# Two gathering layers turned from written-out instructions into hardware loops, with two steps in each PSUM bank

## The reference: what is computed

```python
xn = layernorm(x)
h = elu(gcn(xn, W1, b1)); h = elu(gcn(h, W2, b2))     # gcn: segment_sum((x @ W)[src] * norm, dst) + b
x = x + h + linear_attention(xn)                      # q, k = elu(.) + 1; context = k^T v; projection
x = x + moe(layernorm(x))                             # 8 experts of width 1024, the best 2 for each node
```

## Time and profile before

| | |
|---|---|
| time, median of 3 runs | 3330.49 us (3329.08 to 3338.45) |
| time of the profiled execution | 3338.05 us |
| its span in the profile | 3336.2 us |
| instructions | 45400 |
| TensorE busy | 2378.8 us, 71% |
| TensorE loading weights | 1766.3 us, 53% |
| VectorE busy | 1766.5 us, 53% |
| ScalarE busy | 619.5 us, 19% |
| GpSimd busy | 1965.2 us, 59% |
| DMA | 397.27 MB, mean 119 GB/s |

### The profile page before, as it was taken

One profiled execution on the slowest core, in us unless ns is written; L12 is line 12 of the kernel. 1 busy time (PEld: TensorE's weight loads), 2 busy tenths in 40 slices (PEclk: granted clock), 3 DMA queues, 4 the chain that ended last, 5 costly groups with the idle time before them and its releaser, 6 DMA issues. The chain is left out here.

```text
span 3336.2 us, 45400 instructions
## 1 busy us (share of the span) xinstructions
PE 2378.8 (71%) x10847; PEld 1766.3 (53%) x10847; DVE 1766.5 (53%) x4443; ACT 619.5 (19%) x1318; POOL 1965.2 (59%) x2107
## 2 busy tenths in 40 slices
PE   3367677767677767465666656666669399999998
PEld 2244444444444446243444434444448199999997
DVE  6144444444444456254445545555557766777765
ACT  2000000000000005010001101111116344444443
POOL 1666666666666653666666666666633045555554
PEclk9677877877888788676777777777789599999999
DMA  6333333333333322444444444444422465555551
GB/s 170 114 92 92 90 90 92 92 90 91 88 91 90 89 71 90 116 142 143 141 137 148 145 142 138 146 147 146 145 74 67 146 202 147 146 148 149 148 148 21
DMA packets 177904, 397.27 MB, mean 119 GB/s; under 512 B 42393, under 2 KB 96570, under 8 KB 169514
## 3 DMA queue, kind: packets, MB, share of 16 engines
q0 software_dynamic: 96800, 233.29, 26.9%
q1 hardware_dynamic: 50926, 103.38, 8.6%
q10 hardware_dynamic: 30012, 58.67, 5.1%
HBM read 322.87 MB, written 75.01 MB: 119 GB/s over the span
## 5 line engine op out<-in xcount | busy, mean ns | idle before, releaser
L644 POOL DMA_INDIRECT rows<-rows_layer,srcs x1564 | 1538.4, 984 | 767.6 <-issue 384.3
L705 PE MATMUL l_bank<-rows,sel 128*128 x3332 | 1190.7, 489 | 636.6 <-issue 228.4
L695 DVE TENSOR_TENSOR acc<-acc,l_bank 128x256 f32 x1666 | 699.1, 420 | 1237.2 <-remote 515.9
L705 PEld LDWEIGHTS l_bank<-rows,sel 128*128 128x128 f32 x3332 | 705.3, 236 | 997.2 <-issue 468.8
L1637 PE MATMUL ps_y<-whl,hhi 128*128 128x512 f32 x896 | 320.8, 398 | 0.0
L1593 POOL DMA_INDIRECT out<-ys,g_sum x112 | 182.2, 1627 | 198.1 <-DVE ys L1549 172.9
L673 DVE TENSOR_TENSOR sel<-iota_n,dloc 128x512 f32<-128x512 f32 x418 | 286.7, 686 | 20.1 <-issue 20.1
L1508 ACT ACTIVATE hr<-ffn_bank,vec 128x256 f32<-128x256 f32 x448 | 212.7, 475 | 375.9 <-PE ffn_bank L1449 335.4
L1447 PE MATMUL ffn_bank<-xh,whl 128*128 128x256 f32 x896 | 252.2, 281 | 2.4 <-DVE xl L1523 2.4
L1448 PE MATMUL ffn_bank<-xl,whl 128*128 128x256 f32 x896 | 252.2, 281 | 0.0
L1449 PE MATMUL ffn_bank<-xh,whl 128*128 128x256 f32 x896 | 252.0, 281 | 0.0
(11 more groups left out here) (273 smaller groups left out, 2240.8 us busy)
## 6 DMA issues: line engine op xcount, KB each, us to landing
whl<-w_hi SPq DMA_DIRECT2D x32, 1024.0 KB
whl<-w_lo SPq DMA_DIRECT2D x32, 1024.0 KB
rows<-rows_layer,srcs POOLq DMA_INDIRECT x1564
w_qkv<-wide ACTq DMA_DIRECT2D x49, 335.0 KB
w_hi<-whi ACTq DMA_DIRECT2D x49, 335.0 KB
w_lo<-wlo ACTq DMA_DIRECT2D x49, 335.0 KB
rows_layer<-acc SPq DMA_DIRECT2D x25, 256.0 KB, 2.1
rows_x<-acc SPq DMA_DIRECT2D x7, 910.0 KB
```

The lines of the kernel that those rows point to most:

```text
L644: pool.indirect_dma_start(rows[:, (n + 1) % ROWS, :], None, table[layer], bass.IndirectOffsetOnAxis(ap=srcs[:, n:n + 1], axis=0)).then_inc ...
L695: v.tensor_tensor(to, to, step_bank(s), ALU.add).wait_op(sem(f"summed{layer}"), s + 1, "sem-ge").then_inc(sem(f"added{layer}"), 1)
L705: t.matmul(step_bank(s), sel[:, s % SELS, :], rows_flat[:, bass.ds(slot * D, D)], start=True, stop=True).wait_op(sem(f"here{layer}"), t.to ...
```

## The change

The streams of TensorE, VectorE and SyncE for both layers, and ScalarE's work beside them, become hardware loops. The first turn, the 49th and the last 49 steps stay written out, with turns 2 to 48 in a loop of 16 steps each; SyncE loops over turns of 32 tiles; ScalarE loops over node tiles. Step numbers and the addresses that follow from them are computed in registers. GpSimd's 782 gathers for each layer stay written out.

Two steps share a PSUM bank: its halves hold the results of steps 2m and 2m + 1, so four banks hold eight results. TensorE waits for VectorE only ahead of an even step, until both results of the bank have been added. VectorE's add of an even step waits for both results, and that of an odd step only for the add before. The ring of 0/1 matrices grows from 12 to 16, made 10 steps ahead instead of 6, with three groups of four ahead of the first step.

```diff
--- before.py
+++ after.py
@@ -31,10 +31,12 @@
 PAIRS = -(-NT // 2)
 assert BLOCKS >= 2 * PAIRS + 2
 SG = -(-STEPS // P)
-ROWS, SELS, FOUR = 32, 12, 4
+ROWS, SELS, FOUR = 32, 16, 4
 LOADED = 4
 TURN = 16
 BEHIND, FREED_AT = 16, 8
+FULL_TURNS = (ET - ROWS + BEHIND) // ROWS
+assert ROWS % FREED_AT == 0 and BEHIND % FREED_AT == 0
 assert ROWS > BEHIND and ROWS & (ROWS - 1) == 0 and PAD_DST + NT < 1 << 16 and BLOCKS * D < 1 << 16 and ET < 1 << 16
 HEADS, HD = 8, 32
 NX, HID = 8, 1024
@@ -62,9 +64,11 @@
 WEIGHTS_AT = 9
 LN_EPS = 1e-5
 DEN_MIN = 1e-6
-AHEAD = 6
 PSB = 4
-assert AHEAD >= PSB + 2 and SELS == 3 * FOUR and STEPS <= SG * P - FOUR
+SUMS = 2 * PSB
+AHEAD = SUMS + 2
+assert AHEAD % FOUR == 2 and SELS >= AHEAD + FOUR + 2 and SELS == TURN and TURN % SUMS == 0
+assert STEPS + AHEAD + FOUR <= SG * P
 
 
 def gps_layer(nc, x, src, dst, wqkv, wproj, bproj, gw1, gb1, gw2, gb2, wr, br, wide, vectors, out):
@@ -645,89 +649,126 @@
                                         bass.IndirectOffsetOnAxis(ap=srcs[:, n:n + 1], axis=0)
                                         ).then_inc(sem(f"slot_{n % ROWS}"), 16)
 
-        def steps_until_free(n):
+        def steps_until_free(n, count):
 
             _, regs = nc.values_load_multi_w_load_instructions(
-                words[2:3, n + 1:min(n + FREED_AT, ET - ROWS) + 1, 0], engines=(SP_ENGINE,), min_val=1, max_val=STEPS,
+                words[2:3, bass.ds(n + 1, count), 0], engines=(SP_ENGINE,), min_val=1, max_val=STEPS,
                 skip_runtime_bounds_check_because="the first step of the next tile of edges")
             return list(regs)
 
         def tiles_here(sp, layer):
 
-            until = []
-            for n in range(ET):
-                sp.wait_ge(sem(f"slot_{n % ROWS}"), (n // ROWS + 1 + layer * -(-(ET - n % ROWS) // ROWS)) * 16)
-                sp.sem_inc(sem(f"here{layer}"), 1)
-                m = n - BEHIND
-                if 0 <= m < ET - ROWS:
-                    if m % FREED_AT == 0:
-                        until = steps_until_free(m)
-                    sp.wait_ge(sem(f"summed{layer}"), until[m % FREED_AT])
-                    sp.sem_inc(sem(f"freed{layer}"), 1)
+            def landed(j):
+                return layer * -(-(ET - j) // ROWS)
+
+            def turn(first, many, arrived):
+                until = []
+                for j in range(many):
+                    sp.wait_ge(sem(f"slot_{j}"), arrived(j))
+                    sp.sem_inc(sem(f"here{layer}"), 1)
+                    if isinstance(first, int):
+                        m = first + j - BEHIND
+                        freed, left = 0 <= m < ET - ROWS, ET - ROWS - m
+                    else:
+                        m, freed, left = first + (j - BEHIND), True, FREED_AT
+                    if freed:
+                        if j % FREED_AT == 0:
+                            until = steps_until_free(m, min(FREED_AT, left))
+                        sp.wait_ge(sem(f"summed{layer}"), until[j % FREED_AT])
+                        sp.sem_inc(sem(f"freed{layer}"), 1)
+
+            turn(0, ROWS, lambda j: (1 + landed(j)) * 16)
+            with sp.Fori(1, FULL_TURNS) as k:
+                values = {b: sp.snap(k * 16 + (1 + b) * 16) for b in sorted({landed(j) for j in range(ROWS)})}
+                turn(k * ROWS, ROWS, lambda j: values[landed(j)])
+            for k in range(FULL_TURNS, -(-ET // ROWS)):
+                turn(k * ROWS, min(ROWS, ET - k * ROWS), lambda j: (k + 1 + landed(j)) * 16)
 
         def step_bank(s):
-            return step_ps[s % PSB][:, 0:D]
-
-        def four_selects(v, layer, s):
-
-            v.tensor_tensor(sel[:, s % SELS:s % SELS + FOUR, :], iota_n[:, None, :].to_broadcast([P, FOUR, P]),
-                            dloc[:, s:s + FOUR, None].to_broadcast([P, FOUR, P]), ALU.is_equal
+            return step_ps[s // 2 % PSB][:, s % 2 * D:(s % 2 + 1) * D]
+
+        def four_selects(v, layer, first, k):
+
+            v.tensor_tensor(sel[:, k % SELS:k % SELS + FOUR, :], iota_n[:, None, :].to_broadcast([P, FOUR, P]),
+                            dloc[:, bass.ds(first + k, FOUR), None].to_broadcast([P, FOUR, P]), ALU.is_equal
                             ).then_inc(sem(f"selected{layer}"), 1)
 
-        def blocks_of(s):
+        def blocks_of(first, count):
 
             _, regs = nc.values_load_multi_w_load_instructions(
-                words[1:2, s:min(s + LOADED, STEPS), 0], engines=(DVE_ENGINE,), min_val=0, max_val=(BLOCKS - 1) * D,
+                words[1:2, bass.ds(first, count), 0], engines=(DVE_ENGINE,), min_val=0, max_val=(BLOCKS - 1) * D,
                 skip_runtime_bounds_check_because="a step's tile is one of the step's number or less, by less than the blocks")
             return list(regs)
 
-        def tiles_of(s):
+        def tiles_of(first, count):
 
             _, regs = nc.values_load_multi_w_load_instructions(
-                words[0:1, s:min(s + LOADED, STEPS), 0], engines=(PE_ENGINE,), min_val=1, max_val=ET,
+                words[0:1, bass.ds(first, count), 0], engines=(PE_ENGINE,), min_val=1, max_val=ET,
                 skip_runtime_bounds_check_because="a count of tiles, 1 to ET")
             return list(regs)
 
-        def step_add(v, layer, s, block):
-            if s > 0:
-                v.wait_ge(sem(f"added{layer}"), s)
+        def number(eng, n):
+            return n if isinstance(n, int) else eng.to_reg(eng.snap(n))
+
+        def step_add(v, layer, first, k, block, whole):
             to = acc[:, bass.ds(block, D)]
-            v.tensor_tensor(to, to, step_bank(s), ALU.add).wait_op(sem(f"summed{layer}"), s + 1, "sem-ge"
-                                                                   ).then_inc(sem(f"added{layer}"), 1)
-
-        def step_sum(t, layer, s, here):
+            if k % 2 == 0:
+                until = number(v, first + (k + 2 if whole else k + 1))
+                ins = v.tensor_tensor(to, to, step_bank(k), ALU.add).wait_op(sem(f"summed{layer}"), until, "sem-ge")
+            else:
+                until = number(v, first + k)
+                ins = v.tensor_tensor(to, to, step_bank(k), ALU.add).wait_op(sem(f"added{layer}"), until, "sem-ge")
+            ins.then_inc(sem(f"added{layer}"), 1)
+
+        def step_sum(t, layer, first, k, here):
             slot = t.snap(here & (ROWS - 1))
             t.to_reg(slot)
-            if s < PSB:
-                t.wait_ge(sem(f"selected{layer}"), s // FOUR + 1)
-            else:
-                t.wait_ge(sem(f"added{layer}"), s - PSB + 1)
-            t.matmul(step_bank(s), sel[:, s % SELS, :], rows_flat[:, bass.ds(slot * D, D)], start=True, stop=True
+            if isinstance(first, int) and first + k < SUMS:
+                t.wait_ge(sem(f"selected{layer}"), k // FOUR + 1)
+            elif k % 2 == 0:
+                t.wait_ge(sem(f"added{layer}"), first + (k - SUMS + 2))
+            t.matmul(step_bank(k), sel[:, k % SELS, :], rows_flat[:, bass.ds(slot * D, D)], start=True, stop=True
                      ).wait_op(sem(f"here{layer}"), t.to_reg(here), "sem-ge").then_inc(sem(f"summed{layer}"), 1)
 
+        def vector_turn(v, layer, first, many, between):
+
+            blocks = blocks_of(first, min(LOADED, many))
+            for k in range(many):
+                if k % LOADED == 1 and k + LOADED - 1 < many:
+                    blocks.extend(blocks_of(first + (k + LOADED - 1), min(LOADED, many - k - LOADED + 1)))
+                if k % FOUR == 2 and (not isinstance(first, int) or first + k + AHEAD < STEPS):
+                    four_selects(v, layer, first, k + AHEAD)
+                if k % 2 == 0 and not (isinstance(first, int) and first + k == 0):
+                    v.wait_ge(sem(f"added{layer}"), first + k)
+                step_add(v, layer, first, k, blocks[k], k + 1 < many)
+                between(k)
+
+        def tensor_turn(t, layer, first, many, between):
+
+            tiles = tiles_of(first, min(LOADED, many))
+            for k in range(many):
+                step_sum(t, layer, first, k, tiles[k])
+                if k % LOADED == 1 and k + LOADED - 1 < many:
+                    tiles.extend(tiles_of(first + (k + LOADED - 1), min(LOADED, many - k - LOADED + 1)))
+                between(k)
+
+        def turns(eng, body, layer, between):
+
+            body(eng, layer, 0, TURN, lambda k: between(0, k, True, False))
+            with eng.Fori(1, NT - 1) as i:
+                body(eng, layer, eng.snap(i * TURN), TURN, lambda k: between(i, k, False, False))
+            body(eng, layer, (NT - 1) * TURN, TURN, lambda k: between(NT - 1, k, False, True))
+            body(eng, layer, NT * TURN, STEPS - NT * TURN, lambda k: None)
+
         def vector_steps(v, layer, between):
 
-            blocks = blocks_of(0)
-            for s in range(0, 2 * FOUR, FOUR):
-                four_selects(v, layer, s)
-            for s in range(STEPS):
-                if s % LOADED == 1 and s + LOADED - 1 < STEPS:
```

(50 more changed lines are left out.)

## The result

The changed kernel takes **3367.38 us** (median of 4 runs, 3362.63 to 3375.12), the kernel before 3333.5 (median of 4 runs, 3329.08 to 3338.45) beside it: a ratio of **1.0107** [1.0083, 1.013], 34 us slower. The forecast was 3329 us and no change. The time lies in the range, but on the other side of its middle: rival B's side, with about its price (+28). Three executions far above all others (3541, 9159 and 10105 us) are left out of the ratios further down.

The account below looks back on a forecast made before the run. The prediction took the gathers' own pace, 1.45 us per tile, as the bound. All terms were 0 but the tails' 1.2 us: 3338.05 - 1.2 = 3336.9, then 7.6 lower for the median, 3329 us; range 3160 to 3385.

Parts of the forecast that it names:

- rival B: Register work lengthens pauses where completions come late: +28 us, 3358, or 3385 with word loads exposed; chance 0.29.
- The pace ... is bound to the gathers themselves: Both gathering layers: one tile of edges per 1.45 us, set by the gathers, whatever the consumers' steps or work.
- Numbers in registers: Computed waits and addresses: up to 3.9 us more per VectorE turn of 22.3 us, off the path, 0.
- Loops: Back edges on four engines: 94 on TensorE, 20 us in total, hidden behind its lead of up to eight steps.
- threshold of 20 us per turn: The slower case decides when VectorE's work plus register work passes some 20 us per turn.
- Both signs named for it: Register work wrong: gathers below 178 per 261 us, and VectorE's idle time before adds by "issue" risen.
- Two steps in a bank: TensorE eight steps ahead of VectorE: could hide some 310 us of VectorE's idle time at most; taken as 0.
- Rival A: Four more steps of cover remove GpSimd's slot waits: 3020 in full, 3175 at half; chance 0.18, small gain 0.10.
- The tail: VectorE's steps after each layer's last gather: odd adds start sooner, two tails together gain 1.2 us.
- rival C: Loop back edges stall: 20 us uncovered, 3349, or 412 us with long TensorE waits, 3741; chance 0.03.

Follow-up runs that it names:

- e1_shared: The changed kernel with every loop written out, two steps to a bank kept; ratio 0.998 to the kernel before.
- e5_dve: One step to a bank as in the kernel before, ring of 16, only VectorE's stream a loop; ratio 1.0001 to the kernel before.
- e10_again: Two steps to a bank, all written out, VectorE's waits at the adds against registers worked out just before; ratio 0.9982 to the kernel before.
- r_after: The changed kernel itself, unaltered, measured again beside the kernel before on chip 4; ratio 1.0072.
- e4_pe: One step to a bank as in the kernel before, ring of 16, only TensorE's stream a loop; ratio 1.0015 to the kernel before.

## Why the prediction was wrong

- **"The pace ... is bound to the gathers themselves"** was half right. Eight steps of lead did not shorten it (e1_shared: 1147.7 us in layer 0, where e5_dve, which measures as before, has 1147.5). But it isn't a constant: with pairing and VectorE's loop it rose to (1261.2 - 94.5)/781 = 1.494 us in layer 0. Equal rates in eight stretches showed that steps and busy time don't set it; I took that to mean that nothing on the consumers' side does. Nor is it a constant of this program: at 3029 it is 1.295 us.
- **The step that failed** is "Numbers in registers": "15 + 3.9 is below 22.3: off the path, 0", together with **Loops**, "hidden behind TensorE's lead". Both put VectorE's loop at nothing. The runs showed that with two steps to a bank it costs 0.7% (0.998 to 1.0051, some 24 us), nearly all in layer 0's gathers (+27.4 us), while the same loop with one step to a bank costs nothing (1.0001). A mean over a turn can't say that an engine is off the path where results come in bursts: VectorE idled 1237 us in all, and still its loop made slots come free later. And TensorE's lead covers TensorE's edges; VectorE's stands behind that lead.
- **Which item of the loop costs is open.** The numbers in the waits cost nothing (0.9982). Halving the back edges went with a ratio of 1.0025, but turns right behind a back edge show no more idle time than the others. The register work was probably overrated: VectorE has 9325 instruction records in the trace after and 8194 before, 12 more per looped turn and not 30, though one record of fused register operations can stand for several.
- **Rival B** had the side and the size (+28; measured +34, and +25 and +26 in two later groups). The size was luck: it was worked out from 20% more instructions, and the traces have 7.5% more records (48804 against 45400), which by the same rule give about 10 us; and its threshold of 20 us per turn was not needed. Both signs named for it came, fewer than 178 gathers per 261 us in layer 0 and more idle time before adds by "issue" (149.6 to 216.0 us), but the second tells nothing: e1_shared, without any register work, has 211.9.
- **Two steps in a bank**: 0 was forecast, with 310 as the bound of a gain. The gain is 0.2%, 5 to 7 us. Rival A is out: GpSimd's waits for freed slots, 346.2 us before, are 341.7 (e1_shared) and 349.7 (e10_again) with pairing written out, and 389.2 in the changed kernel.
- **The tail**: 24.7 and 25.7 us for 30.8 and 29.0, 9.4 us less in both together where 1.2 was forecast (these count from the start of the last gather, the prediction from its end). The size was wrong, and it varies from run to run: r_after has 30.0 and 27.6.
- **Back edges that stall** (rival C) are out. TensorE's branches took 0.215 us at the median, 0.700 at most, its idle time fell, and its loop alone costs 0.15% (e4_pe), 5 us. The Trainium skill ("Runtime: NRT & Kernel Launch", "Instruction fetch mechanics") has a taken branch fetch again when its target has left the buffer. Here the fetches fell from 166 packets (68 + 98) to 57 (21 + 36) for all engines, fewer than the 94 back edges of TensorE's loops alone, so the turns were not fetched anew each time.
- **What stays open**: what in VectorE's loop costs, and why only with two steps to a bank; why mostly in layer 0, of which the smaller delay in layer 1 (0.29 us for 0.54) is a hint and no proof; the 0.2% that the other engines' loops add to it (1.0051 to 1.0072), where the intervals overlap; what makes TensorE's and SyncE's semaphores late in some groups; and why all paired versions are 0.1 to 0.2% slower than before at 3029, where the kernel before has no trace.

The best version is pairing without loops: e1_shared at 0.998 and e10_again, the same with registers in the waits, at 0.9982, 5 to 7 us below the kernel before and well below the changed one; at 3029 the latter is 1.0013.

## What to carry to other kernels

Idle time averaged over a period doesn't show that an engine is off the path: where results come in bursts, ask what the engine does in the microsecond in which a burst ends, measure a delay put there, and check in the trace that the delay is there. Two edits that are each free can cost together, so a change of several parts is to be taken apart in pairs too, and each ratio is to be taken with the kernel before beside it, since the same chip number gave 3357 and 3030 us for it within a quarter of an hour. A deeper buffer behind results that come late moved little here: 0.2%.

## What the hardware showed

The same program took 3351.78 us in one group of measurements (chip 13) and 3034.72 in another (chip 15), 9.5% less, with equal median durations of its gathers. Of the 309 us by which the spans differ, 307 lie in the two layers (gathers 1141.9 and 1140.2 us against 1011.6 and 1008.5, tails 29.8 and 30.7 against 7.4 and 7.9), where TensorE's results and SyncE's waits come late in the one and not in the other. The kernel before differs in the same way (3357 to 3367 and 3029), and on chip 13 both were measured (3357 and 3030). The changed kernel with its transposes moved loses 0.9% at 3357 and 0.1% at 3029; the changed kernel itself was not run at 3029.
